# First layer of an expert tile with the tile's rows stationary: a copy on VectorE and four transposes in place of eight small products

## The chip, the cores and the metric

The kernel runs on one core of one Trainium2 chip. The metric is the time of one execution in microseconds, the median of several. The kernel before takes 1520.85 us (three runs, 1519.32 to 1523.46).

## The reference

One layer of a graph network over 6250 nodes of 256 features, everything in fp32: a sparse sum over 106250 edges, a linear attention over all nodes, and then the part that the change is in, a mixture of 16 experts of which each node takes two.

```python
xn = _layernorm(x, axis=-1)
x = x + _L0_gnn_ref(xn, src, dst, edge_weight, L0_gnn_weight) + _L0_mix_ref(xn[None], Wqkv, Wout, bout)[0]
...
gate_logits = x @ gate_w + gate_b
topk_vals, topk_idx = jax.lax.top_k(gate_logits, K)
topk_w = jax.nn.softmax(topk_vals, axis=-1)
h = jax.nn.relu(jnp.einsum('bsh,ehf->bsef', x, w1) + b1)
expert_out = jnp.einsum('bsef,efh->bseh', h, w2) + b2
sel = jnp.take_along_axis(expert_out, topk_idx[:, :, :, None], axis=2)
moe = jnp.sum(topk_w[..., None] * sel, axis=2)
y = x + moe
```

The experts' layers are 256 to 512 and 512 to 256. Their input is the layer-normed result of the first half.

## The kernel before

**The edges.** The 106250 edges lie in 70 batches of 12 tiles of 128. For each tile GpSimd issues one indirect DMA (L855) that gathers 128 rows of the normed table into `ring`, which holds two batches. TensorE sums a batch in `edges` (L1512) as soon as it has landed, ScalarE copies the sum (L992), TensorE puts it in place (L1521), VectorE adds it (L1116). GpSimd may gather batch b only when batch b-2 has been summed, so a late TensorE holds GpSimd up.

**The other work between batches.** `plan()` (L147) sets, once and by costs written in the code, what each engine does in the slot after each batch: attention (`kv`), the closing of node tiles (`mix`, `gate`), routing (`rank`, `slots`, `line`, `list`), the tiles of the experts (`moe`), and the final sum of node tiles (`fin1`, `fin2`). Each engine walks through the same slots in the same order. For an expert tile the plan counts 3.9 us of TensorE (L136).

**The expert tiles.** Routing gives each pair of a node and an expert a slot in a table in HBM; GpSimd scatters the rows there (L833), 128 slots of one expert make a tile. The tiles come in runs, one run after each routing: runs 0 to 4 (8, 16, 16, 16 and 12 tiles) and the first 13 tiles of run 5 lie between batches, the other 15 tiles of run 5 and the 25 of run 7 after the last batch; the short runs 6 and 8 are left out if they are empty. For tile g, in TensorE's order:

- `xg_turn(g + 1)`, L1636: two transposes of the next tile's rows; ScalarE copies them to SBUF (`xg_copy`, L946);
- `layer1(g)`, L1648: for each of the 4 blocks of 128 hidden features 2 products of 128 columns, the weights stationary and the transposed rows moving. So the result lies in PSUM already turned, features on the partitions, in one of two banks `hps`;
- `layer2(g - 1)`, L1661: 4 products of 256 columns with the turned hidden rows `hT` stationary.

ScalarE's `relu` (L967) adds the bias and makes `hT` (two buffers) from `hps`, in four instructions, as soon as layer 1 is done. VectorE adds the second bias (`moe_y`, L1445), and ScalarE issues the store of the result (`store_y`, L952). SyncE loads a tile's rows (L720) and, if the expert is another than three tiles before, both weights (L732 when `relu` three tiles before is done, L734 when `moe_y` is). Near the end of a part a tile can be empty (`where_taken`, L628): then its products and its `relu` are skipped.

**The end.** When the tiles of the first 42 node tiles are done, GpSimd picks their results out of HBM (`pick`, L846) and `fin1` (L1463 to L1475) and `fin2` (L1484 to L1493) close two node tiles at a time on VectorE. In `fin2` VectorE needs a square root that ScalarE makes (L986) and that stands in ScalarE's order behind the tile before it. The plan weaves 17 such pairs among the 25 tiles of run 7; 8 pairs follow after the last tile.

```python
            def moe(r, j):
                ...
                layer1(r, j)
                if j:
                    layer2(r, j - 1)
                if j + 1 == n:
                    layer2(r, j)
```

Of the kernel before, what the change touches and what calls it, by code (L numbers as in the profile page):

```python
# [9 lines left out]
ACT = mybir.ActivationFunctionType  # L10
AX = mybir.AxisListType

P = 128
N = 6250
D = 256
KD = D // P
# [25 lines left out]
E, F = 16, 512  # L42
FC = F // P
TS = 128
# [57 lines left out]
RUNS, VISITS = runs()  # L102
# [5 lines left out]
WB = 3  # L108
# [245 lines left out]
def gps_layer(nc, x, src, dst, first_dst, edge_w, gnn_w, wkv, wq, wout, bout, gate_w, gate_b,  # L354
# [5 lines left out]
    with ExitStack() as ctx:  # L360
# [3 lines left out]
        def sem(name):  # L364
            return ctx.enter_context(nc.semaphore(name))
# [30 lines left out]
        take = carve(room[:, :])  # L396
# [8 lines left out]
        take = carve(room[:, :])  # L405
        w1_sb = [take(W1ROW) for _ in range(WB)]
        w2_sb = [take(W2BROW) for _ in range(WB)]
        hT = [take(FC, TS) for _ in range(2)]
        xg = [take(D) for _ in range(XB)]
        xgT = [take(KD, TS) for _ in range(2)]  # L410

# [101 lines left out]
        gate_cols = [wide[1][:, 512 + D + i * E:512 + D + (i + 1) * E] for i in range(6)]  # L513
        mT, gnnT = [sq[:, i * 512:(i + 1) * 512].rearrange("p (j n) -> p j n", j=KD) for i in range(2)]
        boutT = ks[0][:, 0:D].rearrange("p (j n) -> p j n", j=KD)
        hps = [ps[:, 5, :], ps[:, 1, :]]
        xgps = ps[:, 6, 0:KD * TS]
        ops = ps[:, 7, 0:D]

# [73 lines left out]
        w1_in = sems("w1_in", WB)  # L593
        w2_in = sems("w2_in", WB)
        l1_done = sem("l1_done")
        relu_done = sem("relu_done")
        l2_done = sem("l2_done")
        y_done = sem("y_done")
# [12 lines left out]
        def after(eng, s, n):  # L611

            if n > 0:
                eng.wait_ge(s, n)
# [27 lines left out]
        def skip(eng, done, g0, n, each=1):  # L642

            if n:
                after(eng, done, each * g0)
                eng.sem_inc(done, each * n)
# [218 lines left out]
        def _(act):  # L865
# [88 lines left out]
            def moe(r, j):  # L954
                s, g0, n, _ = RUNS[r]
                g = g0 + j
                if j == 0:
                    act.wait_ge(listed, LISTS[s])
                    xg_copy(g)
                if j + 1 < n:  # L960
                    xg_copy(g + 1)

                def relu():
                    act.wait_ge(l1_done, g + 1)
                    after(act, l2_done, g - 1)
                    for f in range(FC):
                        last = act.activation(hT[g % 2][:, f, :], hps[g % 2][:, f * TS:(f + 1) * TS], ACT.Relu,  # L967
                                              bias=w1_sb[g % WB][:, KD * F + f:KD * F + f + 1])
                    last.then_inc(relu_done, 1)
                where_taken(act, r, j, relu, relu_done)  # L970
                if j:
                    store_y(r, j - 1)
                if j + 1 == n:
                    store_y(r, j)
# [22 lines left out]
        def _(dve):  # L997
# [443 lines left out]
            def moe_y(g):  # L1441
# [2 lines left out]
                after(dve, ys_out[g % 2], 16 * (g // 2))  # L1444
                dve.tensor_tensor(yo[g % 2], ops, w2_sb[g % WB][:, W2ROW:], ALU.add).then_inc(y_done, 1)  # L1445

            def moe(r, j):
                _, g0, n, _ = RUNS[r]
                if j:
                    moe_y(g0 + j - 1)  # L1450
                if j + 1 == n:
                    moe_y(g0 + j)

            def left_out(r):
                skip(dve, y_done, RUNS[r][1], RUNS[r][2])

            def fin1(f):
# [46 lines left out]
        def _(pe):  # L1504
# [134 lines left out]
            def layer1(r, j):  # L1639
                g = RUNS[r][1] + j  # L1640

                def products():
                    pe.wait_ge(xg_copied, g + 1)
                    after(pe, relu_done, g - 1)
                    pe.wait_ge(w1_in[g % WB], 16 * (g // WB + 1))
                    for f in range(FC):
                        for k in range(KD):
                            mm = pe.matmul(hps[g % 2][:, f * TS:(f + 1) * TS], w1_sb[g % WB][:, k * F + f * P:k * F + (f + 1) * P],  # L1648
                                           xgT[g % 2][:, k, :], start=(k == 0), stop=(k == KD - 1))
                    mm.then_inc(l1_done, 1)  # L1650
                where_taken(pe, r, j, products, l1_done)

            def layer2(r, j):
                g = RUNS[r][1] + j

                def products():
                    pe.wait_ge(relu_done, g + 1)
                    after(pe, y_done, g)
                    pe.wait_ge(w2_in[g % WB], 16 * (g // WB + 1))
                    for f in range(FC):  # L1660
                        mm = pe.matmul(ops, hT[g % 2][:, f, :], w2_sb[g % WB][:, f * D:(f + 1) * D], start=(f == 0), stop=(f == FC - 1))  # L1661
                    mm.then_inc(l2_done, 1)
                where_taken(pe, r, j, products, l2_done)

            def moe(r, j):
                s, g0, n, _ = RUNS[r]
                if j == 0:
                    pe.wait_ge(listed, LISTS[s])
                    xg_turn(g0)
                if j + 1 < n:  # L1670
                    xg_turn(g0 + j + 1)
                layer1(r, j)
                if j:
                    layer2(r, j - 1)
                if j + 1 == n:
                    layer2(r, j)

            def left_out(r):
                _, g0, n, _ = RUNS[r]
                skip(pe, xg_turned, g0, n)  # L1680
                skip(pe, l1_done, g0, n)
                skip(pe, l2_done, g0, n)

            pe.wait_ge(pool_consts, POOL_CONSTS)
# [78 lines left out]
```

## Time and profile before

| | us |
|---|---|
| median of 3 runs | 1520.85 |
| span of the profiled execution (its whole time is not given) | 2053.1 |
| of it PE busy / PE weight loads / DVE / ACT / POOL | 1168.8 / 848.9 / 651.8 / 406.3 / 1005.6 |
| last gather of an edge batch issued at | 1730.0 |
| layer 1 (L1648), 1904 passes, busy | 279.8 |
| layer 2 (L1661), 952 passes, busy | 270.5 |
| bytes moved by DMA | 323.09 MB |

PE is TensorE, PEld its weight loads, DVE VectorE, ACT ScalarE, POOL GpSimd, SP SyncE; a q behind a name is the engine's queue of DMA issues. An fp32 product shows as two passes: 119 tiles x 8 products are 1904 rows of L1648. A transpose shows as one. The profiled execution is 532 us longer than the runs without a profile.

### The profile page before, as it was taken

How to read it: one execution, taken by the hardware profiler on the slowest of the kernel's cores; microseconds unless marked ns; L12 is line 12 of the kernel's file. 1: busy time of each engine (PE TensorE's matmuls, PEld its weight loads, DVE VectorE, ACT ScalarE, POOL GpSimd, SP SyncE). 2: the span in 40 equal slices, each digit the busy share in tenths (PEclk: the TensorE clock that was granted, in tenths of full speed). 3: DMA queues.
4: the chain of work that ended last, by engine and by line, in shares of the span. 5: the costliest groups of instructions: out<-in, count | busy, mean ns of one | idle time of the engine just before them, and what ended most of it. 6: DMA issues, size and time to landing. Idle time of an engine off the chain costs nothing. (4 is left out here: it accounts for less than half of the span.)

```text
span 2053.1 us, 23292 instructions
## 1 busy us (share of the span) xinstructions
PE 1168.8 (57%) x6546; PEld 848.9 (41%) x6546; DVE 651.8 (32%) x2406; ACT 406.3 (20%) x1093; POOL 1005.6 (49%) x1094
## 2 busy tenths in 40 slices
PE   0278888976423767432576324773266367576681
PEld 0144444544313655221554213552154156465670
DVE  7144344333632212223112131122212222412568
ACT  4033232321101312000211001210021022222221
POOL 2746666664365244566254663446624643204634
PEclk9899999987755888655788666887577588887885
DMA  9345444432134656233574325653364274366784
GB/s 329 97 151 185 154 153 155 141 90 62 47 98 153 217 187 216 80 91 117 176 238 143 90 92 183 196 178 90 121 220 162 85 265 143 124 210 217 244 256 138
DMA packets 155049, 323.09 MB, mean 157 GB/s; under 512 B 24769, under 2 KB 97729, under 8 KB 154785
## 3 DMA queue, kind: packets, MB, share of 16 engines
q1 hardware_dynamic: 65760, 148.16, 21.9%
q0 software_dynamic: 49296, 134.68, 21.6%
q10 hardware_dynamic: 39856, 38.67, 5.6%
q8 instruction: 57, 0.93, 0.2%
q14 instruction: 80, 0.65, 0.1%
HBM read 257.06 MB, written 64.36 MB: 157 GB/s over the span
## 5 line engine op out<-in xcount | busy, mean ns | idle before, releaser
L855 POOL DMA_INDIRECT ring<-normed_rows,src_sb x831 | 797.9, 960 | 780.0 <-PE ps L1512 462.2
L1661 PE MATMUL ps<-room 128*128 128x256 f32 x952 | 270.5, 435 | 115.9 <-issue 79.9
L1648 PE MATMUL ps<-room 128*128 128x128 f32 x1904 | 279.8, 300 | 70.3 <-issue 58.6
L1648 PEld LDWEIGHTS ps<-room 128*128 128x128 f32 x1904 | 260.4, 214 | 80.0 <-issue 75.2
L1661 PEld LDWEIGHTS ps<-room 128*128 128x128 f32 x952 | 199.8, 221 | 155.4 <-issue 85.3
L1445 DVE TENSOR_TENSOR desk<-ps,room 128x256 f32<-128x256 f32 x121 | 51.3, 424 | 587.6 <-PE ps L1661 293.4
L1512 PE MATMUL ps<-ring,S 128*32 128x256 f32 x1680 | 145.6, 453 | 153.0 <-DVE aggT L1116 77.9
L1539 PE MATMUL ps<-room,tT 128*128 128x512 f32 x392 | 196.7, 644 | 11.4 <-issue 11.1
L967 ACT ACTIVATE room<-ps,room 128x128 f32<-128x128 f32 x476 | 136.1, 369 | 303.5 <-remote 201.2
L846 POOL DMA_INDIRECT ring<-results_by_slot,slot_i x98 | 96.5, 984 | 146.4 <-issue 80.9
L1512 PEld LDWEIGHTS ps<-ring,S 128*32 128x32 f32 x1680 | 60.8, 125 | 211.8 <-issue 188.4
L833 POOL DMA_INDIRECT rows_by_slot<-X,slot_i x98 | 96.1, 981 | 103.0 <-DVEq L1337 74.7
L1521 PE MATMUL ps<-Pm,accs 128*128 128x128 f32 x280 | 55.3, 329 | 138.1 <-ACT accs L992 106.2
L1529 PE MATMUL ps<-ident,X 128*128 128x128 f32 x196 | 48.7, 333 | 140.9 <-ACT tT L881 95.2
L992 ACT COPY accs<-ps 128x256 f32<-128x256 f32 x70 | 26.3, 376 | 495.4 <-remote 339.4
L1539 PEld LDWEIGHTS ps<-room,tT 128*128 128x128 f32 x392 | 77.5, 209 | 98.6 <-issue 98.5
L1133 DVE TENSOR_REDUCE kv_var<-room 128x16 f32<-128x1024 f32 x49 | 59.7, 1218 | 179.0 <-ACT room L901 130.3
L1636 PE MATMUL ps<-ident,room 128*128 128x128 f32 x242 | 53.6, 307 | 105.5 <-ACT room L946 69.3
L1521 PEld LDWEIGHTS ps<-Pm,accs 128*128 128x128 f32 x280 | 46.4, 227 | 156.5 <-ACT accs L992 120.3
L1529 PEld LDWEIGHTS ps<-ident,X 128*128 128x128 f32 x196 | 25.1, 161 | 166.2 <-ACT tT L881 103.6
L946 ACT COPY room<-ps 128x256 f32<-128x256 f32 x121 | 44.7, 370 | 235.2 <-remote 94.9
L1636 PEld LDWEIGHTS ps<-ident,room 128*128 128x128 f32 x242 | 33.5, 156 | 125.4 <-issue 115.8
(226 smaller groups left out, 1247.0 us busy)
## 6 DMA issues: line engine op xcount, KB each, us to landing
room<-in_w2b SPq DMA_DIRECT2D x92, 640.0 KB
room<-in_w1b SPq DMA_DIRECT2D x92, 514.0 KB
room<-rows_by_slot SPq DMA_DIRECT2D x121, 128.0 KB
results_by_slot<-desk ACTq DMA_DIRECT2D x121, 128.0 KB
rows_by_slot<-desk ACTq DMA_DIRECT2D x6, 2432.0 KB
ring<-normed_rows,src_sb POOLq DMA_INDIRECT x831
normed_rows<-X SPq DMA_DIRECT2D x7, 896.0 KB, 8.0
result<-ring SPq DMA_DIRECT2D x49, 128.0 KB
```

Source lines behind the costliest of these rows:

```text
L833: pool.indirect_dma_start(out=xs[p], out_offset=bass.IndirectOffsetOnAxis(ap=slot_i[:, k, q:q + 1], axis=0), in_=X2[:, q, :], in_offset=No ...
L846: pool.indirect_dma_start(out=pk[i][k][:, n, :], out_offset=None, in_=ys[p], in_offset=bass.IndirectOffsetOnAxis(ap=slot_i[:, k, q:q + 1], ...
L855: pool.indirect_dma_start(out=ring[:, b % 2 * BT + m, :], out_offset=None, in_=table, in_offset=bass.IndirectOffsetOnAxis(ap=src_sb[:, b * ...
L967: last = act.activation(hT[g % 2][:, f, :], hps[g % 2][:, f * TS:(f + 1) * TS], ACT.Relu, bias=w1_sb[g % WB][:, KD * F + f:KD * F + f + 1])
L1133: dve.tensor_reduce(kv_var[q % 2][:, :], sq.rearrange("p (h d) -> p h d", d=DH), AX.X, ALU.add).then_inc(kv_var_done, 1)
L1512: mm = pe.matmul(acc[w * W:(w + 1) * W, :], S[b % 2][:, m, :], ring[:, b % 2 * BT + m, :], start=(t == 0), stop=(t == GT - 1), skip_group_ ...
L1521: mm = pe.matmul(placed[:, k * P:(k + 1) * P], accs[:, k * P:(k + 1) * P], Pm[b % 2][:, :], start=True, stop=True, skip_group_check=True)
L1529: mm = pe.transpose(tps[:, k * P:(k + 1) * P], rows[:, k * P:(k + 1) * P], ident[:])
L1539: mm = pe.matmul(wide[q % 2][:, h * 512:(h + 1) * 512], tT[n % 2][:, k * P:(k + 1) * P], wkv_sb[:, k, h * 512:(h + 1) * 512], start=(k == ...
L1636: mm = pe.transpose(xgps[:, k * TS:(k + 1) * TS], xg[g % XB][:, k * P:(k + 1) * P], ident[:])
L1648: mm = pe.matmul(hps[g % 2][:, f * TS:(f + 1) * TS], w1_sb[g % WB][:, k * F + f * P:k * F + (f + 1) * P], xgT[g % 2][:, k, :], start=(k == ...
L1661: mm = pe.matmul(ops, hT[g % 2][:, f, :], w2_sb[g % WB][:, f * D:(f + 1) * D], start=(f == 0), stop=(f == FC - 1))
```

## The change

Layer 1 is turned round: the tile's transposed rows are stationary and the weight rows move, 512 columns at a time, so that 2 products take the place of 8. Their result has the tile's rows on the partitions. VectorE copies it from PSUM to SBUF (`h_copy`), TensorE turns it back with four transposes (`h_turn`), and `relu` works on what they leave. `hps`, `hT` and the new buffers are single. In the slot of a tile TensorE's order becomes `xg_turn(g + 1)`, `layer1(g)`, `layer2(g - 1)`, `h_turn(g)`; VectorE's `h_copy(g)` stands ahead of `moe_y(g - 1)`. The copy, the transposes and `relu` are done for an empty tile too.

```diff
+        hps = ps[:, 5, 0:F]
+        hTps = ps[:, 1, 0:FC * TS]
...
 # ScalarE, moe
-                def relu():
-                    act.wait_ge(l1_done, g + 1)
-                    after(act, l2_done, g - 1)
-                    for f in range(FC):
-                        last = act.activation(hT[g % 2][:, f, :], hps[g % 2][:, f * TS:(f + 1) * TS], ACT.Relu,
...
-                where_taken(act, r, j, relu, relu_done)
+                act.wait_ge(h_turned, g + 1)
+                after(act, l2_done, g)
+                for f in range(FC):
+                    last = act.activation(hT[:, f, :], hTps[:, f * TS:(f + 1) * TS], ACT.Relu,
+                                          bias=w1_sb[g % WB][:, KD * F + f:KD * F + f + 1])
+                last.then_inc(relu_done, 1)
...
 # VectorE
+            def h_copy(g):
+                dve.wait_ge(l1_done, g + 1)
+                after(dve, h_turned, g)
+                dve.tensor_copy(h_rows, hps).then_inc(h_copied, 1)
+
             def moe(r, j):
                 _, g0, n, _ = RUNS[r]
+                h_copy(g0 + j)
                 if j:
                     moe_y(g0 + j - 1)
...
 # TensorE, layer 1
-                    after(pe, relu_done, g - 1)
+                    after(pe, h_copied, g)
                     pe.wait_ge(w1_in[g % WB], 16 * (g // WB + 1))
-                    for f in range(FC):
-                        for k in range(KD):
-                            mm = pe.matmul(hps[g % 2][:, f * TS:(f + 1) * TS], w1_sb[g % WB][:, k * F + f * P:k * F + (f + 1) * P],
-                                           xgT[g % 2][:, k, :], start=(k == 0), stop=(k == KD - 1))
+                    for k in range(KD):
+                        mm = pe.matmul(hps, xgT[g % 2][:, k, :], w1_sb[g % WB][:, k * F:(k + 1) * F],
+                                       start=(k == 0), stop=(k == KD - 1))
...
+            def h_turn(g):
+                pe.wait_ge(h_copied, g + 1)
+                after(pe, relu_done, g)
+                for f in range(FC):
+                    mm = pe.transpose(hTps[:, f * TS:(f + 1) * TS], h_rows[:, f * P:(f + 1) * P], ident[:])
+                mm.then_inc(h_turned, 1)
...
                 if j:
                     layer2(r, j - 1)
+                h_turn(g0 + j)
                 if j + 1 == n:
                     layer2(r, j)
```

TensorE's order at the first tile after the last routing's list, in run 5, before (L1636 turns the next tile's rows, L1648 is layer 1, L1661 layer 2 of the tile before):

```order
L1636 MATMUL ps<-ident,room 128x128 [waits xg_copied,xg_in2]
L1636 MATMUL ps<-ident,room 128x128
L1648 MATMUL ps<-room 128x128 [waits w1_in1,relu_done,xg_copied]
L1648 MATMUL ps<-room 128x128 x7
L1661 MATMUL ps<-room 128x256 [waits w2_in0,y_done,relu_done]
L1661 MATMUL ps<-room 128x256 x3
```

and with the change (L1645 turns the rows, L1656 is layer 1, L1676 layer 2, L1665 the new transposes):

```order
L1645 MATMUL ps<-ident,room 128x128 [waits xg_copied,xg_in2]
L1645 MATMUL ps<-ident,room 128x128
L1656 MATMUL ps<-room 128x512 [waits w1_in1,h_copied,xg_copied]
L1656 MATMUL ps<-room 128x512
L1676 MATMUL ps<-room 128x256 [waits w2_in0,y_done,relu_done]
L1676 MATMUL ps<-room 128x256 x3
L1665 MATMUL ps<-ident,room 128x128 [waits relu_done,h_copied]
L1665 MATMUL ps<-ident,room 128x128 x3
```

Between layer 2 and the next tile's transposes TensorE now waits for VectorE's copy. VectorE's order among the last tiles with `fin2` and `fin1` between two results, before (L1445 is `moe_y`):

```order
L1445 TENSOR_TENSOR desk<-ps,room 128x256 [waits ys_out1,w2_in0,l2_done]
L1484 SCALAR_TENSOR_TENSOR ring<-ring,f_mv,gamma_b 128x256 [waits f_stats]
L1484 SCALAR_TENSOR_TENSOR ring<-ring,f_mv,gamma_b 128x256
L1487 RECIPROCAL f_r<-f_r 128x2 [waits f_std]
L1493 SCALAR_TENSOR_TENSOR ring<-ring,f_r,aggT 128x256 [waits f_scaled,f_recip]
L1493 SCALAR_TENSOR_TENSOR ring<-ring,f_r,aggT 128x256 [waits f_scaled]
L1445 TENSOR_TENSOR desk<-ps,room 128x256 [waits ys_out0,w2_in1,l2_done]
```

and with the change (L1452 is the copy, L1447 `moe_y`):

```order
L1452 COPY room<-ps 128x512 [waits h_turned,l1_done]
L1447 TENSOR_TENSOR desk<-ps,room 128x256 [waits ys_out1,w2_in2,l2_done]
L1493 SCALAR_TENSOR_TENSOR ring<-ring,f_mv,gamma_b 128x256 [waits f_stats]
L1493 SCALAR_TENSOR_TENSOR ring<-ring,f_mv,gamma_b 128x256
L1496 RECIPROCAL f_r<-f_r 128x2 [waits f_std]
L1502 SCALAR_TENSOR_TENSOR ring<-ring,f_r,aggT 128x256 [waits f_scaled,f_recip]
L1502 SCALAR_TENSOR_TENSOR ring<-ring,f_r,aggT 128x256 [waits f_scaled]
```

The copy stands behind all closing work of the slot before. ScalarE's order at the same place, before (L967 is `relu`, L986 the root for `fin2`):

```order
L946 COPY room<-ps 128x256 [waits l1_done,xg_turned]
L967 ACTIVATE room<-ps,room 128x128 [waits l2_done,l1_done]
L967 ACTIVATE room<-ps,room 128x128 x3
L950 TENSOR_LOAD ttab
L950 ISA x2
L952 ISA [waits y_done]
L952 DMA results_by_slot<-desk 128x256
L986 ACTIVATE f_r<-f_mv,eps_t 128x2 [waits f_stats]
```

and with the change:

```order
L950 COPY room<-ps 128x256 [waits l1_done,xg_turned]
L970 ACTIVATE room<-ps,room 128x128 [waits l2_done,h_turned]
L970 ACTIVATE room<-ps,room 128x128 x3
L954 TENSOR_LOAD ttab
L954 ISA x2
L956 ISA [waits y_done]
L956 DMA results_by_slot<-desk 128x256
L988 ACTIVATE f_r<-f_mv,eps_t 128x2 [waits f_stats]
```

The order is the same, but the root stands behind a `relu` that now waits for the transposes, and so for layer 2 of the tile before.

## Rows read from the trace of the kernel before

**Rows 1.** The page's first line.

```profile
span 2053.1 us, 23292 instructions
```

**Rows 2.** One line: the gathers; ns min/median/max, first and last start.

```profile
L855 POOL DMA_INDIRECT ring<-normed_rows,src_sb x831: 940/947/2857, 53.5 to 1730.0; - x167
```

**Rows 3.** The page's groups: the scatters; busy us, mean ns, idle before.

```profile
L833 POOL DMA_INDIRECT rows_by_slot<-X,slot_i x98 | 96.1, 981 | 103.0 <-DVEq L1337 74.7
```

**Rows 4.** Who waited for whom, whole span: us, times, longest.

```profile
POOL ring L855 <- PE ps L1512: 462.2, 40, 32.4
```

**Rows 5.** Timeline, PE and POOL: start, us, engine, [idle before].

```profile
1031.02 0.27 PE L1648 MATMUL ps<-room 128*128 128x128 f32 x1 [1.04 <-issue]
...
1033.90 0.37 PE L1648 MATMUL ps<-room 128*128 128x128 f32 x1 [1.05 <-issue]
...
1045.82 0.94 POOL L855 DMA_INDIRECT ring<-normed_rows,src_sb  x1 [0.30 <-issue]
```

**Rows 6.** Timeline, one undisturbed tile of run 5 after the last batch.

```profile
1803.73 0.38 PE L1636 MATMUL ps<-ident,room 128*128 128x128 f32 x2
...
1803.95 1.95 PE L1648 MATMUL ps<-room 128*128 128x128 f32 x16
...
1805.73 1.89 PE L1661 MATMUL ps<-room 128*128 128x256 f32 x8
...
1805.93 1.14 ACT L967 ACTIVATE room<-ps,room 128x128 f32<-128x128 f32 x4 [0.57 <-PE ps L1648]
...
1807.46 0.38 PE L1636 MATMUL ps<-ident,room 128*128 128x128 f32 x2
```

**Rows 7.** Timeline, attention: eight passes of 512 columns and what follows.

```profile
274.56 3.60 PE L1539 MATMUL ps<-room,tT 128*128 128x512 f32 x8
...
278.00 1.05 PE L1547 MATMUL ps<-room 128*128 128x128 f32 x8
```

**Rows 8.** One line: VectorE on 512 columns of PSUM.

```profile
L1125 DVE TENSOR_TENSOR room<-ps,kv_s x49: 690/691/692, 109.1 to 447.8; 128x512 f32<-128x512 f32 x49
```

**Rows 9.** Timeline, PE at a batch of edges among tiles.

```profile
1019.19 1.50 PE L1512 MATMUL ps<-ring,S 128*32 128x256 f32 x24
1020.62 0.44 PE L1636 MATMUL ps<-ident,room 128*128 128x128 f32 x2
...
1024.41 0.61 PE L1521 MATMUL ps<-Pm,accs 128*128 128x128 f32 x4
1024.86 0.38 PE L1636 MATMUL ps<-ident,room 128*128 128x128 f32 x2
```

**Rows 10.** Stretches: busy us, clock, DMA share, GB/s.

```profile
710.00:720.00 10.00, 9.91 (x74) 9.43 (x75) 0.64 (x2) 4.43 (x15) 0.00 (x0) 1.00 0.94 328
...
1843.00:2004.00 161.00, 110.25 (x635) 96.67 (x635) 76.33 (x227) 40.39 (x137) 74.37 (x76) 0.83 0.75 240
```

**Rows 11.** Timeline, from the end of run 5 to run 7.

```profile
1836.10 1.97 PE L1661 MATMUL ps<-room 128*128 128x256 f32 x8 [0.34 <-DVE desk L1445]
...
1842.96 0.34 SPq L732 DMA_DIRECT2D room<-in_w1b  x1
...
1849.86 0.45 PE L1636 MATMUL ps<-ident,room 128*128 128x128 f32 x1 [11.80 <-DMA room<-rows_by_slot]
```

**Rows 12.** Timeline, a tile of run 7 with `fin2` and `fin1`.

```profile
1957.12 0.42 DVE L1445 TENSOR_TENSOR desk<-ps,room 128x256 f32<-128x256 f32 x1 [1.26 <-PE ps L1661]
...
1957.47 0.87 DVE L1484 SCALAR_TENSOR_TENSOR ring<-ring,f_mv,gamma_b 128x256 f32<-128x256 f32 x2
...
1958.14 0.29 ACT L986 ACTIVATE f_r<-f_mv,eps_t 128x2 f32<-128x2 f32 x1 [1.60 <-DVE desk L1445]
...
1958.47 0.17 DVE L1487 RECIPROCAL f_r<-f_r 128x2 f32<-128x2 f32 x1
```

**Rows 13.** The chain that ended last: two starts of `fin2`, one pair apart.

```profile
2016.56 0.55 DVE ring L1484 x2
...
2020.93 0.55 DVE ring L1484 x2
```

More of the change, by code:

```diff
@@ L407, in gps_layer @@
         w2_sb = [take(W2BROW) for _ in range(WB)]
-        hT = [take(FC, TS) for _ in range(2)]
+        hT = take(FC, TS)
+        h_rows = take(F)
         xg = [take(D) for _ in range(XB)]
@@ L515, in gps_layer @@
         boutT = ks[0][:, 0:D].rearrange("p (j n) -> p j n", j=KD)
-        hps = [ps[:, 5, :], ps[:, 1, :]]
+        hps = ps[:, 5, 0:F]
+        hTps = ps[:, 1, 0:FC * TS]
         xgps = ps[:, 6, 0:KD * TS]
@@ L595, in gps_layer @@
         l1_done = sem("l1_done")
+        h_copied = sem("h_copied")
+        h_turned = sem("h_turned")
         relu_done = sem("relu_done")
@@ L961, in moe @@
                     xg_copy(g + 1)
-                def relu():
-                    act.wait_ge(l1_done, g + 1)
-                    after(act, l2_done, g - 1)
-                    for f in range(FC):
-                        last = act.activation(hT[g % 2][:, f, :], hps[g % 2][:, f * TS:(f + 1) * TS], ACT.Relu,
-                                              bias=w1_sb[g % WB][:, KD * F + f:KD * F + f + 1])
-                    last.then_inc(relu_done, 1)
-                where_taken(act, r, j, relu, relu_done)
+                act.wait_ge(h_turned, g + 1)
[4 more added lines that the diff above has]
+                last.then_inc(relu_done, 1)
                 if j:
@@ L1454, in left_out @@
             def left_out(r):
+                skip(dve, h_copied, RUNS[r][1], RUNS[r][2])
                 skip(dve, y_done, RUNS[r][1], RUNS[r][2])
@@ L1660, in products @@
                     for f in range(FC):
-                        mm = pe.matmul(ops, hT[g % 2][:, f, :], w2_sb[g % WB][:, f * D:(f + 1) * D], start=(f == 0), stop=(f == FC - 1))
+                        mm = pe.matmul(ops, hT[:, f, :], w2_sb[g % WB][:, f * D:(f + 1) * D], start=(f == 0), stop=(f == FC - 1))
                     mm.then_inc(l2_done, 1)
@@ L1681, in left_out @@
                 skip(pe, l1_done, g0, n)
+                skip(pe, h_turned, g0, n)
                 skip(pe, l2_done, g0, n)
```

## The prediction

> **What bounds the kernel now.** I read the page, then the waits, then the timeline of single tiles, then stretches with the DMA share, and last the chain that ended last.
>
> The span is 2053.1 us [rows 1], 532 us more than the median of 1520.85. The timeline shows why the two differ: again and again TensorE starts one small pass and then sits for about a microsecond with no releaser [rows 5], though all operands are there. In undisturbed stretches nothing of this kind occurs. So I take every price from undisturbed stretches, keep the profile's stalls out of the sum, and add the sum to the median.
>
> Up to the last gather GpSimd sets the floor. A gather takes 0.95 us and follows the one before by 0.30 us [rows 2, 5], so 1.25 us each. From 53.5 us on come 831 gathers and 84 of the 98 scatters [rows 2, 3]: 53.5 + 915 x 1.25 = 1197 us, while the profile has its last gather at 1730.0 [rows 2]. The 462.2 us for which GpSimd waited for TensorE [rows 4] are mostly the stalls, passed on. What is left of the median is 324 us; the profile has 323 us behind the last gather, with stalls in it. So perhaps 50 to 75 us of real waits lie before the last gather, the rest is the end phase: 15 tiles of run 5, 25 of run 7 with the closing pairs, then pure closing on VectorE, 4.37 us a pair [rows 13].
>
> An undisturbed tile takes 1807.46 - 1803.73 = 3.73 us of TensorE: 0.22 for two transposes, 1.78 for layer 1 (16 passes of 0.111), 1.73 for layer 2 [rows 6]. A batch of edges takes 1.43 and 0.45 us [rows 9]. Three tiles and a batch are 13.1 us against 12 x 1.25 = 15.0 on GpSimd: TensorE has 1.9 us spare. The DMA engines have none: with tiles back to back they are 94% busy at 328 GB/s without any gather beside [rows 10].
>
> **Layer 1 and the transposes on TensorE.** Eight passes of 512 columns take 278.00 - 274.56 = 3.44 us, 0.43 each [rows 7]. The new layer 1 has 4: 1.72 us in place of 1.78. As many columns stream as before (4 x 512, 16 x 128), and the weight loads were hidden already. The four transposes take 4 x 0.11 = 0.44 us at the pitch of L1636 [rows 6]. Net +0.37 us a tile, 4.10 in place of 3.73.
>
> The trace's 0.43 us for a 512-column pass is 4 times its 0.11 for 128. The Trainium skill (TensorE: Matmul & The Clock Gate, Back-to-back issue gap) gives, for a stream of load and product, about 81 ns at 128 columns and 131 ns at 512; by that layer 1 would fall from 1.30 to 0.52 us and the change would win 0.45 us a tile even with its transposes at 81 ns. The rows contradict it for fp32, so the sum goes by the rows.
>
> **The copy on VectorE.** The trace has no plain copy of 512 columns from PSUM; VectorE's work of that size takes 0.69 us [rows 8], and 256 columns take 0.42 [rows 12]. I take 0.69, between 0.42 and 0.69. With VectorE idle it hides under layer 2 of the tile before (1.73 us). The same holds for `relu`: it now starts after the transposes, 1.14 us [rows 6], and has 0.22 + 1.72 us until the next layer 2. So among tiles without closing work only the 0.37 us shows.
>
> **SyncE.** The w1 load three tiles on waits for `relu`, which is now about 1.2 us later than the `moe_y` for which the w2 load ahead of it in the queue waits. The lead of this load falls from about 7.2 to 7.0 us of a period that has grown to 12.3. I count nothing; its cover is the two tiles' weights already queued. ScalarE's store of the result stands behind `relu` too, about 1.1 us later, covered by the second `yo`.
>
> **Sum by stretch.**
> - Before the last gather, 81 tiles. 13.1 + 3 x 0.37 = 14.2 us is still under 15.0, and the weights queue at the DMA engines. Cost only where TensorE is late already: the five to seven tiles at the head of each of 5 bursts, and waits for the copy behind `gate`. Bounds 0 and 81 x 0.37 + 5 x 3 = 45; I take 5, near the covered end, because both covers show in rows.
> - Run 5 after the last gather: 13 tiles x 0.37 = 5.
> - End of run 5: two empty tiles, for which nothing was done after the last layer 2 [rows 11]. Now two rounds of transposes (0.44) with a `relu` (1.14 and handover) between them stand ahead of SyncE's loads for run 7, for which TensorE waits 11.8 us [rows 11]: +3. The first tile of run 7 has no layer 2 to hide the copy: +1.
> - Run 7 with closing work. Now VectorE needs 4.37 + 0.42 = 4.8 us for a tile with a full pair [rows 12, 13], about 4.3 on the mean over the pattern (two full pairs, a `fin2`, a `fin1` in four tiles). But 161 us x 240 GB/s = 38.6 MB move there [rows 10], at 328 GB/s 118 us, 4.9 us a tile: the DMA engines bound it. With the change three engines stand in a ring. The copy comes after all closing work of the slot before; then transposes 0.45, `relu` 1.19, the store's issue 0.6, the root 0.33 until VectorE can go on with the reciprocal: 2.6 us, where now it is 1.35 from `moe_y`'s start and 0.8 of it worked [rows 12]. A full pair then takes 0.7 + 2.6 + 3.57 (a pair without its first 0.8) = 6.9 us. Stepping through four tiles gives 22.5 us, 5.6 a tile, 24 tiles 134 us. Against 118: +16; against 24 x 4.3: +31; if the DMA engines still hide it, 0. I take 15, since the DMA bound is the one that rows show.
> - Last tile: its `relu` and transposes are bare, 0.44 + 1.3: +2. The 8 closing pairs after it stay.
>
> Sum 5 + 5 + 3 + 1 + 15 + 2 = +31 us: **1552 us**.
>
> **Rivals.**
> 1. *Covered, not slower.* The DMA engines hold run 7 and the bursts at more than 4.9 us a tile, and each copy falls into a wait. It decides this way if the ring (5.6 by my stepping) in truth takes 4.9 or less, as it would if the closing pairs catch up in the slots without one. Then only end effects of a few us stay, partly made up: 1521 to 1525. For it: 94% DMA share at full pitch [rows 10]. Against: over run 7 the share is 0.75, stalls included. Chance 0.13.
> 2. *The gathers are held too.* The 50 to 75 us of waits before the last gather are TensorE's lateness, not DMA. Then 81 x 0.37 and the waits behind `gate` and at heads of runs come in full: +45 in place of 5, and run 7 at +16: 1592; half-way 1572. For it: GpSimd waits for TensorE alone [rows 4]. Against: 14.2 us fits into 15.0. Chance 0.20.
> 3. *Faster.* The transposes run while TensorE waits for weights, so that only layer 1's 0.06 us counts: 119 x 0.06 = 7 us, 1514. It needs TensorE idle just where the copy is ready, in all stretches, and no ring at the closing pairs. Chance 0.05. The rule of the Trainium skill on the issue gap would carry it further; the trace speaks against it.
>
> **How the numbers follow.** The forecast (1530 to 1572) has 0.62, the rivals 0.13, 0.20 and 0.05. A measurement of this kernel tells about 0.3%, 4.6 us, from no change. Faster 0.05, same 0.13, slower 0.82. The range goes from 1522, which leaves out the third and part of the first rival, to 1588, which leaves out the far end of the second.
>
> **What would show it.** Right: L1648's 1904 rows become 476 of about 0.43 us pitch; four new transposes of 0.11; a copy of about 0.69 us, 121 times; an undisturbed tile at 4.1 us; in run 7 VectorE waits about 1 us for the root between the two parts of `fin2`, and TensorE waits for the copy ahead of its transposes. The profile's span may fall though the time grows, since its stalls go with TensorE's rows and a tile has fewer. Wrong: a tile still at 3.7 us; no wait for the copy in run 7; a time under 1525 would say that the DMA engines or GpSimd cover all, one over 1575 that the gathers are held.

## The result and the profile after

The changed kernel takes 1568.77 us (median of 4 runs, 1568.12 to 1571.03), the kernel before beside it on the same chip 1522.15 us (4 runs, 1519.32 to 1525.73). The ratio is 1.0294, with a 95% interval of 1.0263 to 1.0325: 45 us slower, where 31 were forecast. The direction was right, the time lies inside the range, and the forecast is 17 us too low. One run of all those told of here was slow (1596.09 us, in experiment 12), and no ratio counts it, though the median there does.

The profiled execution of the changed kernel has no stalls: its span is 1566.8 us, 2 us below the median. So its stretches can be read as they are. For those of the kernel before, a second profiled execution without stalls was taken in the first experiment (span 1524.4). From here on "before" means that one.

The page's groups, first of the changed kernel (line engine op, shapes | busy us, mean ns | idle before it, releaser):

```profile
L1656 PE MATMUL ps<-room 128*128 128x512 f32 x476 | 250.9, 654 | 6.9 <-DMA room<-in_w1b 4.3
L1452 DVE COPY room<-ps 128x512 f32<-128x512 f32 x121 | 83.2, 688 | 249.5 <-PE ps L1656 248.9
```

then of before:

```profile
L1648 PE MATMUL ps<-room 128*128 128x128 f32 x1904 | 257.8, 294 | 26.7 <-DMA room<-in_w1b 26.1
```

The 1904 passes are 476, and they save 6.9 us of busy time. The copy takes 688 ns. The last number of each row of layer 1 tells how close the DMA engines were: before, TensorE waited 26.1 us for w1 weights at this line, now 4.3. The four transposes a tile, as one answer on their line shows them (min/median/max ns, who it waited for, us and times):

```profile
L1665 PE MATMUL ps<-ident,room x484: 272/273/477, 499.9 to 1522.1; 128*128 128x128 f32 x162
...
  DVE room L1452: 70.1, 40
```

The gathers, which answer to [rows 2], end later, and GpSimd waits more for TensorE ([rows 4] show the stalled profile). Of the changed kernel, the line of the gathers, then who waited for whom over the whole span:

```profile
L859 POOL DMA_INDIRECT ring<-normed_rows,src_sb x831: 940/946/2865, 53.7 to 1268.3; - x167
...
POOL ring L859 <- PE ps L1521: 62.6, 15, 15.7
```

and of before:

```profile
L855 POOL DMA_INDIRECT ring<-normed_rows,src_sb x831: 941/946/2858, 53.4 to 1254.1; - x167
...
POOL ring L855 <- PE ps L1512: 44.6, 10, 16.3
```

From the starts of such instructions each profile can be cut in stretches: to the last gather, to the last `moe_y` of run 5 (the 96th), to the first turned rows of run 7, to the last `moe_y`, to the end.

| us | last gather at | rest of run 5 | to run 7 | run 7 | closing | span |
|---|---|---|---|---|---|---|
| before | 1254.1 | 97.8 | 9.6 | 121.8 | 41.1 | 1524.4 |
| changed | 1268.3 | 107.0 | 10.4 | 139.9 | 41.2 | 1566.8 |
| difference | +14.2 | +9.2 | +0.8 | +18.1 | +0.1 | +42.4 |
| forecast | +5 | +5 | +4 | +17 | 0 | +31 |

Each row is one profiled execution. Profiles of the experiments below that have the same form in a stretch tell how far it scatters: the last gather lies at 1250.2 to 1255.7 in the old form (experiments 1, 4 and 10) and at 1268.3 to 1273.3 in the new one (the changed kernel, 2, 6 and 9), run 7 takes 121.2 to 123.7 us in the old form and 139.9 to 142.2 in the new one. So the first difference is 13 to 23 us, and nothing under about 2.5 us in run 7 can be told from scatter.

Run 7 of the changed kernel, as [rows 10] show it of before: stretch, us, busy of each engine, granted clock, DMA share, GB/s. The second stretch holds two tiles with a pair.

```profile
1385.00:1525.00 140.00, 116.72 (x449) 75.60 (x450) 93.51 (x257) 41.36 (x142) 73.86 (x77) 0.91 0.86 274
...
1452.00:1465.00 13.00, 9.06 (x40) 5.95 (x39) 10.73 (x31) 3.27 (x12) 9.96 (x11) 1.00 0.68 201
```

The same stretch of before:

```profile
1361.00:1483.00 122.00, 102.48 (x650) 91.72 (x650) 78.58 (x232) 41.76 (x142) 72.89 (x76) 0.95 0.92 313
```

Without stalls the kernel before has its DMA engines 92% busy at 313 GB/s through all of run 7; TensorE has time over there. Changed, TensorE's granted clock over run 7 is 0.91 in place of 0.95 (the last section comes back to it), and the DMA share falls to 0.86 and in the tiles with pairs to 0.68: something else has become the bound. The timeline of one such tile, which answers to [rows 12], shows what: VectorE (DVE), ScalarE (ACT) and TensorE (PE) follow each other in a ring.

```profile
1452.33 0.60 PE L1665 MATMUL ps<-ident,room 128*128 128x128 f32 x4
...
1452.97 0.88 ACT L970 ACTIVATE room<-ps,room 128x128 f32<-128x128 f32 x3 [2.60 <-PE ps L1665]
...
1453.65 0.34 ACTq L956 DMA_DIRECT2D results_by_slot<-desk  x1
...
1454.05 0.30 ACT L988 ACTIVATE f_r<-f_mv,eps_t 128x2 f32<-128x2 f32 x1
...
1454.37 0.17 DVE L1496 RECIPROCAL f_r<-f_r 128x2 f32<-128x2 f32 x1 [0.63 <-ACT f_r L988]
...
1457.83 0.67 DVE L1452 COPY room<-ps 128x512 f32<-128x512 f32 x1
...
1458.56 0.66 PE L1665 MATMUL ps<-ident,room 128*128 128x128 f32 x4 [1.97 <-DVE room L1452]
...
1460.66 0.17 DVE L1496 RECIPROCAL f_r<-f_r 128x2 f32<-128x2 f32 x1 [1.04 <-ACT f_r L988]
...
1464.85 0.66 PE L1665 MATMUL ps<-ident,room 128*128 128x128 f32 x4 [1.97 <-DVE room L1452]
```

The transposes start `relu`, the root stands behind `relu` and the store, VectorE waits for the root, works off the pair, and only then makes the next copy, for which TensorE sits 1.97 us. One round is 1464.85 - 1458.56 = 6.29 us. Over run 7, from the first tile's turned rows to the last's in the same list of starts, a tile takes 5.3 us (before: 4.6).

### The profile page after: what moved, and what is told of

It reads as the page before. It is cut to its first block and busy times, and to the rows that moved or that the text cites. A ratio compares the mean times of both kernels' runs of the same rounds, so it can differ in the third digit from the quotient of the medians.

```text
span 1566.8 us, 21700 instructions
## 1 busy us (share of the span) xinstructions
PE 1093.6 (70%) x5602; PEld 699.5 (45%) x5602; DVE 732.6 (47%) x2527; ACT 411.3 (26%) x1101; POOL 1003.7 (64%) x1094
## 3 DMA queue, kind: packets, MB, share of 16 engines
q0 software_dynamic: 49296, 134.68, 27.5%
## 5 line engine op out<-in xcount | busy, mean ns | idle before, releaser
L1521 PE MATMUL ps<-ring,S 128*32 128x256 f32 x1680 | 132.0, 457 | 178.8 <-DMA ring<-normed_rows,src_sb 121.6
L1656 PE MATMUL ps<-room 128*128 128x512 f32 x476 | 250.9, 654 | 6.9 <-DMA room<-in_w1b 4.3
L1676 PE MATMUL ps<-room 128*128 128x256 f32 x952 | 229.9, 385 | 8.5 <-ACT room L970 8.4
L1676 PEld LDWEIGHTS ps<-room 128*128 128x128 f32 x952 | 184.7, 195 | 87.9 <-issue 42.7
L1452 DVE COPY room<-ps 128x512 f32<-128x512 f32 x121 | 83.2, 688 | 249.5 <-PE ps L1656 248.9
L1548 PE MATMUL ps<-room,tT 128*128 128x512 f32 x392 | 182.3, 609 | 0.0
L1656 PEld LDWEIGHTS ps<-room 128*128 128x128 f32 x476 | 89.7, 210 | 75.2 <-issue 71.9
L1645 PE MATMUL ps<-ident,room 128*128 128x128 f32 x242 | 53.4, 306 | 80.7 <-issue 45.2
L1447 DVE TENSOR_TENSOR desk<-ps,room 128x256 f32<-128x256 f32 x121 | 51.3, 424 | 120.1 <-PE ps L1676 118.6
L1548 PEld LDWEIGHTS ps<-room,tT 128*128 128x128 f32 x392 | 73.6, 198 | 73.8 <-issue 73.8
L1665 PE MATMUL ps<-ident,room 128*128 128x128 f32 x484 | 76.6, 283 | 28.5 <-DVE room L1452 27.1
L1665 PEld LDWEIGHTS ps<-ident,room 128*128 128x128 f32 x484 | 60.5, 144 | 52.9 <-DVE room L1452 43.0
L905 ACT ACTIVATE room<-ps 128x1024 f32<-128x1024 f32 x49 | 50.2, 1024 | 124.4 <-PE ps L1548 124.4
L1645 PEld LDWEIGHTS ps<-ident,room 128*128 128x128 f32 x242 | 31.0, 153 | 92.6 <-issue 71.9
```

The costliest lines, as they stand in the source:

```text
L1452: dve.tensor_copy(h_rows, hps).then_inc(h_copied, 1)
L1521: mm = pe.matmul(acc[w * W:(w + 1) * W, :], S[b % 2][:, m, :], ring[:, b % 2 * BT + m, :], start=(t == 0), stop=(t == GT - 1), skip_group_ ...
L1548: mm = pe.matmul(wide[q % 2][:, h * 512:(h + 1) * 512], tT[n % 2][:, k * P:(k + 1) * P], wkv_sb[:, k, h * 512:(h + 1) * 512], start=(k == ...
L1645: mm = pe.transpose(xgps[:, k * TS:(k + 1) * TS], xg[g % XB][:, k * P:(k + 1) * P], ident[:])
L1656: mm = pe.matmul(hps, xgT[g % 2][:, k, :], w1_sb[g % WB][:, k * F:(k + 1) * F], start=(k == 0), stop=(k == KD - 1))
L1665: mm = pe.transpose(hTps[:, f * TS:(f + 1) * TS], h_rows[:, f * P:(f + 1) * P], ident[:])
```

## The experiments

Each is compared with runs of the kernel before on the same chip; differences in us are its ratio less 1, times the median of before there. The plain differences of the two medians lie up to 2.4 us off these.

**1. The kernel before again, for a profile without stalls.** No edit.

> The kernel before, unchanged, profiled again, to have a profile without the stalls of TensorE that lengthened the first one by 532 us. Expected by every theory: 1520 to 1526 us, and in the profile a span near it. The theory that DMA bounds run 7 expects its 25 tiles to take about 118 to 125 us with waits for loads in them; the theory that VectorE and TensorE bound it expects about 24 x 4.3 = 103 us plus few waits. The theory that the gathers are already held by TensorE expects GpSimd's waits for L1512 to sum to 50 us or more.

Measured: ratio 0.9989 (0.9966 to 1.0012), span 1524.4 at a median of 1526.05. The stalls were a property of the first profiled execution. The last gather is at 1254.1, against the floor of 1197 in the prediction. Run 7 takes 121.8 us at a DMA share of 0.92, as the theory that DMA bounds it expects. GpSimd waits 44.6 us for the sums of edges, just under the 50 that the theory of held gathers asked for: it was held for most of the 57 us above the floor, and the run decides for neither side alone.

**2 to 4. The new form in some runs only.** Three kernels with both forms, chosen by run: the head has the new form in runs 0 to 4, the middle in 5 and 6, the last in 7 and 8.

```diff
+TURNED_RUNS = (0, 1, 2, 3, 4)
...
+                if r in TURNED_RUNS:
+                    h_copy(g0 + j)
```

and the same choice at `relu`, `layer1`, `h_turn` and `layer2`.

> Only the tiles of runs 0 to 4 (68 tiles, all before the last gather) take the new form; later tiles have the old one. Ring theory (the loss is in run 7, where the copy, relu and the root for the closing pairs stand in a ring): +5 to +13 us. Rival (TensorE already holds the gathers, and 0.37 us a tile comes in full there): +25 us or more. Everything covered before the last gather: 0.

> Only the tiles of run 5 (13 before the last gather, 15 after it, two of them empty) and of the left-out run 6 take the new form. Both theories: 13 x 0.37 = 5 us after the last gather, 3 for the two empty tiles, 1 to 3 before it: +8 to +11 us.

> Only the 25 tiles of run 7 (and the left-out run 8) take the new form. Ring theory: +18 to +33 us, the largest of the three parts, with full closing pairs at 6.2 us a tile where the kernel before has 4.8. Rival: 25 x 0.37 + 3 = +12 us. If the sum of the three parts is the whole +46, the parts are independent.

Measured: head 1.0086 (1.0061 to 1.0112), +13 us; middle 1.0049 (1.0031 to 1.0067), +7.5; last 1.0102 (1.0073 to 1.0130), +15.6. Together 36 us of the 45 (by plain medians 42 of 47); each part is known to 3 to 4 us, so whether the parts add up to the whole is known to several us only. The last is below its expectation of 18 to 33, and its interval of 11 to 20 us holds the rival's 12 too; it is the profile that tells them apart, and that is of the slowest of its six runs. The profiles put the time where the new form is: the head has its last gather at 1268.5 and all else within 1.5 us of before, the last has run 7 at 142.2 us (+20.4) and all else within 1.6. So the loss before the last gather is not a consequence of anything later. The middle's profile shows the rest of run 5 at 111.8 us, 4.8 more than the changed kernel has there, with a span of 1540.5 against a median of 1536.03; how exactly its term is to be split stays open by a few us.

**5. The transposes alone.** The kernel before, with four more transposes a tile after layer 2, into the free bank; their result is not used. No copy, no new wait.

```diff
                 if j:
                     layer2(r, j - 1)
+                after(pe, relu_done, g0 + j)
+                for f in range(FC):
+                    pe.transpose(hps[(g0 + j + 1) % 2][:, f * TS:(f + 1) * TS], upper[:], ident[:])
```

> The kernel before, with four more transposes (of a constant, into the bank that is free until the next tile) at the end of each tile's slot on TensorE: 0.44 us of TensorE a tile and no new wait for another engine. What it adds to the computation is not used. If TensorE's time as such is small (GpSimd covers it before the last gather, the DMA engines cover it in run 7), then 13 to 15 x 0.44 = 6 us in run 5, 0 to 4 elsewhere: +6 to +10 us. If TensorE's time per tile is what the change costs, 119 x 0.44 = +52 us, or at least +20.

Measured: 1539.82 us, ratio 1.0086 (1.0056 to 1.0115), +13 us, more than the theory gave. By stretch: last gather at 1266.8 (+12.7), rest of run 5 101.6 (+3.8), run 7 120.9 (-0.9), closing the same. This is the most telling run. Before the last gather bare TensorE time brings nearly all of the changed kernel's +14.2. In run 7 the same transposes, 25 x 0.44 = 11 us of TensorE, cost nothing that can be told from scatter: the waits for the DMA engines give way. A part is given back by the clock, 0.98 there against 0.95 before; TensorE is busy 110.32 us over the 121, 7.8 more than before. What run 7 loses with the change, +18.1, is therefore the copy, its waits, and the clock that TensorE loses in them.

**6. The root ahead of `relu`.** The changed kernel, with ScalarE's root for `fin2` ahead of the tile in the last slot.

```diff
+            roots_first = list(SLOTS[NB])
+            for i in range(1, len(roots_first)):
+                if roots_first[i][0] == "fin2" and roots_first[i - 1][0] == "moe":
+                    roots_first[i - 1:i + 1] = [roots_first[i], roots_first[i - 1]]
```

> The changed kernel, but after the last gather ScalarE makes the root for fin2 ahead of the tile (its copy and relu) that stands before it in the plan. Ring theory: VectorE's 16 waits for the root in run 7 (15.6 us in the changed kernel's trace) go, and most of it comes back: 1557 to 1562 us. Rival, that the copy's place behind the closing work alone decides: the wait moves to the next copy, under 3 us come back.

Measured: 1557.66 us, ratio 1.0199 (1.0168 to 1.0230), 11 us less than the change by the medians and 14 by the ratios, within what the theory of the ring expected. Run 7 takes 128.3 us, +6.5 instead of +18.1; the stretches ahead of it are not faster (last gather 1270.7). Cutting one link of the ring gives back 12 us of the 18.

**7. The copy on ScalarE.** The changed kernel, with `h_copy` ahead of `relu` on ScalarE instead of on VectorE.

```diff
+                act.wait_ge(l1_done, g + 1)
+                after(act, h_turned, g)
+                act.copy(h_rows, hps).then_inc(h_copied, 1)
...
-                h_copy(g0 + j)
```

> The changed kernel, with the copy of 512 columns on ScalarE (0.59 us) in place of VectorE, ahead of relu in its order. Theory that TensorE's loss is the wait for a copy queued behind gate and behind the closing pairs on VectorE: TensorE's 70 us of weight-load waits for the copy go; 8 to 10 us come back before the last gather and 6 to 10 in run 7: 1548 to 1556 us. Rival (TensorE's own 0.37 us a tile): nothing comes back, 1567 or more.

Measured: 1546.19 us, ratio 1.0149 (1.0121 to 1.0176), 22 us less than the change. More came back than the 14 to 20 us expected, and elsewhere: 16 us in run 7, which takes 123.9 (+2.1), and only 3 before the last gather, which is at 1265.4 (+11.3); the rest of run 5 takes 103.7 (+5.9). TensorE had waited 23.5 us for the copy before the last gather, and these waits cost little there. The copy takes less on ScalarE too, and TensorE's wait for it goes. The groups of this kernel, as above:

```profile
L969 ACT COPY room<-ps 128x512 f32<-128x512 f32 x121 | 70.9, 586 | 112.5 <-PE ps L1658 111.9
...
L1667 PE MATMUL ps<-ident,room 128*128 128x128 f32 x484 | 73.2, 274 | 8.0 <-ACT room L969 7.9
```

In run 7 it is mainly what the copy is queued behind that costs: ScalarE has nothing long ahead of it. This run also takes 0.69 us a tile of work off VectorE and does not part the two. Experiment 6 bounds that: the copy is still VectorE's there, and run 7 is 4.4 us longer than here. The new buffers and `hps` and `hT` are single in this run as well, so whatever that costs in run 7 lies within its +2.1.

**8. Both.** The copy on ScalarE and the root ahead of `relu`.

> The changed kernel with both: the copy on ScalarE and the root ahead. If both waits are parts of one ring in run 7, the two together bring back less than their sum: 1543 to 1550 us; what is left over the kernel before is TensorE's 0.37 us a tile in run 5, the empty tiles and the bare ends of runs, 15 to 20 us. If they are independent: 1538 or less.

Measured: 1550.27 us, ratio 1.0163 (1.0138 to 1.0189): no better than experiment 7, and not the 1538 of independent waits. The times of 7 and 8 differ by less than their intervals, but in the profiles run 7 takes 131.0 us here, 7 more. With the root first, ScalarE waits for VectorE's variance before it may copy. Who waited for whom in run 7 (us, times, longest), of experiment 8:

```profile
ACT f_r L992 <- DVE f_mv L1490: 29.8, 14, 3.1
...
PEld ps L1671 <- ACT room L969: 17.5, 16, 2.2
```

and of experiment 7:

```profile
DVE f_r L1498 <- ACT f_r L992: 6.2, 8, 2.0
PEld ps L1667 <- ACT room L969: 1.8, 2, 1.5
```

The wait for the copy is 17.5 us in one and 1.8 in the other, though the copy is on the same engine: the root that was moved ahead holds it.

**9. Empty tiles skipped.** The changed kernel, with the transposes and `relu` of an empty tile under `where_taken`, as before the change.

```diff
+                def relu():
...
+                where_taken(act, r, j, relu, relu_done)
...
+                where_taken(pe, r, j, turns, h_turned)
```

> The changed kernel, with the transposes and relu of an empty tile skipped as the products are (the copy stays). Expected by every theory: the two empty tiles at the end of run 5 cost 3 us there, so 1564 to 1567 us, and the stretch from the last result of run 5's full tiles to run 7's first rows as in the kernel before. If it is still 1569, the end of run 5 was not on the path.

Measured: 1571.11 us, ratio 1.0293 (1.0264 to 1.0321): no gain, against 2 to 5 us expected. The stretch between run 5 and run 7 is 9.3 us instead of 10.4, so the term is worth about 1 us in this stretch, too little for the time to show.

**10. The root ahead in the kernel before.**

> The kernel before with the same move of ScalarE's root as in the changed kernel: its VectorE waits for the root only once, 1.4 us, so nothing to win: 1519 to 1526 us. A gain of over 5 us would say that the place of the root costs by itself, whatever the form of layer 1.

Measured: 1524.51 us, ratio 0.9993 (0.9973 to 1.0014), run 7 at 121.2 us. Before the change there is no ring to cut: VectorE waits 1.4 us for the root in all of run 7, the changed kernel 15.6.

**11 and 12. Where before the last gather do the transposes cost?** Experiment 5 with its transposes in some tiles only.

```diff
+                if 1 <= r <= 4 and j < 9:
```

in 11, and in 12

```diff
+                if r == 0 or (1 <= r <= 4 and j >= 9):
```

> The kernel before with the four extra transposes in only the first nine tiles of runs 1 to 4 (36 tiles, 15.8 us of TensorE). Theory: the transposes of the earlier run cost time before the last gather only where TensorE is already behind GpSimd, at the heads of the runs, where the mixing products (5.1 us) stand among the tiles. Then these 36 tiles bring most of the 12.7 us that all tiles brought before the last gather: last gather 1259 to 1265, time +7 to +11 us. Rival: each tile costs alike wherever it stands, 12.7 x 36 / 81 = +5.6 us, last gather 1258 or less. Second rival: the cost lies in the last tiles of the runs, then +0 to +3.

> The kernel before with the four extra transposes in all tiles of run 0 and the tiles from the tenth on in runs 1 to 4 (32 tiles, 14.1 us of TensorE), and in no others. By the theory of the heads these are nearly hidden by GpSimd's gathers: last gather 1252 to 1258, time +0 to +4 us, of which up to 3 in run 0. Rival that each tile costs alike: 12.7 x 32 / 81 = +5.0 us. Rival that the ends of the runs cost: +7 to +10.

Measured: heads 1532.73 us, 1.0041 (1.0011 to 1.0070), +6.2 us, last gather in the profile 1254.2; the others 1534.49 us, 1.0046 (1.0015 to 1.0077), +7.0 us, last gather 1262.6. The theory of the heads is not borne out: both last gathers lie outside what it expected, on the side against it. By the ratios each tile costs about alike, 0.2 us of its 0.44, as the first rival expected, and the two sum to the 13 of experiment 5; but the intervals (+2 to +11 and +2 to +12 us) are wide enough for the other theories, so that alike is the likeliest and not shown. The profile of the heads does not show its +6; it is of the fastest of its ten runs, and the last gather scatters by some 5 us from profile to profile.

Where the gathers are held shows batch by batch, in the time from a batch's first gather to the next one's (us; numbers are the batches'):

| batch | before | changed | transposes alone | 11, heads | 12, others |
|---|---|---|---|---|---|
| 28 | 20.6 | 27.5 | 24.9 | 21.6 | 26.7 |
| 31 | 15.0 | 18.7 | 18.3 | 16.4 | 16.4 |
| 44 | 15.1 | 17.9 | 15.9 | 15.1 | 17.0 |
| 55 | 15.0 | 16.7 | 17.0 | 15.1 | 15.2 |

Of the 69 spacings 57 differ by less than 0.5 us between before and the change. So most slots are covered, as the prediction had it; the loss is in a few. The four rows shown make 15.1 us; the others beyond 0.5 us go both ways (the largest, batch 66 with +2.9, spreads from 17.4 to 20.9 us among kernels without the new form). Batch 28 waits for a sum of edges that stands in TensorE's order behind run 0 and the first tiles of run 1; run 0 is in experiment 12, and so is most of this loss (its 26.7; without the new form there it spreads from 20.3 to 23.6, in experiments 10 and 4). Batch 31 falls in a slot with mixing products. TensorE there, before:

```profile
592.66 1.08 PE L1612 MATMUL ps<-gnn_sb,aggT 128*128 128x272 f32 x4
593.57 0.61 PE L1521 MATMUL ps<-Pm,accs 128*128 128x128 f32 x4
594.02 0.38 PE L1636 MATMUL ps<-ident,room 128*128 128x128 f32 x2
...
605.31 1.50 PE L1512 MATMUL ps<-ring,S 128*32 128x256 f32 x24
```

and changed, from one batch of edges to the next:

```profile
593.76 1.50 PE L1521 MATMUL ps<-ring,S 128*32 128x256 f32 x24
595.19 0.44 PE L1538 MATMUL ps<-ident,X 128*128 128x128 f32 x2
...
596.37 1.15 PE L1618 MATMUL ps<-M,tT 128*128 128x288 f32 x4
597.35 1.08 PE L1621 MATMUL ps<-gnn_sb,aggT 128*128 128x272 f32 x4
...
600.15 0.61 PE L1530 MATMUL ps<-Pm,accs 128*128 128x128 f32 x4
...
613.23 0.66 PE L1665 MATMUL ps<-ident,room 128*128 128x128 f32 x4 [0.61 <-DVE room L1452]
613.82 1.50 PE L1521 MATMUL ps<-ring,S 128*32 128x256 f32 x24
```

This slot holds 600.15 - 595.19 = 4.96 us of mixing products beside the three tiles. It takes 20.06 us of TensorE, against 15.0 for GpSimd's twelve gathers. With the two slots before it (14.33 each, from the same lines' starts) TensorE needs 48.7 us for three batches where GpSimd needs 45: the 3.7 us by which batch 31 is longer. Before, the same three slots take TensorE 13.69, 13.23 and 18.14, which is 45.05 us: there was no slack to hide anything in.

## Why the prediction was right in sign and short in size

**Prices.** Right. Layer 1 is four passes with a pitch of 0.43 us: in the timeline it starts at 1452.98 and layer 2 follows at 1454.70, 1.72 us. The transposes take 0.44, the copy 0.688 (0.69 forecast), and an undisturbed tile 4.10 us, between 1448.23 and 1452.33 on line L1665. The rule of the Trainium skill (TensorE: Matmul & The Clock Gate, Back-to-back issue gap), by which 512 columns go at about 131 ns, does not hold for these fp32 passes: with 512 columns streaming, layer 1 still takes 0.43 us a pass.

**Before the last gather: 5 taken, 14.2 measured.** This is the step that failed. The prediction compared "13.1 + 3 x 0.37 = 14.2 us" of TensorE with 15.0 of GpSimd and found it covered. That batch of 13.1 us has no other work in it; slots with mixing products take 5 us more, and from run 0 on sums of edges are late already (GpSimd idles 5.9 us ahead of batch 29 before the change, 12.8 after it). What stands in its place is measured: the transposes alone bring +12.7 here, and the head runs of the new form +14.4. The other part of the term, waits for the copy behind `gate`, is there with 23.5 us, but moving the copy to ScalarE gives only 3 us back. "Near the covered end" was the wrong place in the bounds of 0 and 45; the second rival had the mechanism, with 45 far too much and its half-way point of 1572 close to the result.

**Run 5 behind the last gather: 5 and 3 taken, 9.2 measured.** 3.8 of it is transposes (experiment 5), near the 5. Between 1311 and 1315 there is a wait that the prediction did not have in this stretch: the copy stands on VectorE behind the routing chain. The chain's last step ahead of the copy, the copy and the transposes of the changed kernel:

```profile
1314.06 0.17 DVE L1342 TENSOR_TENSOR prob<-prob 128x7 f32<-128x7 f32 x1
1314.16 0.69 DVE L1452 COPY room<-ps 128x512 f32<-128x512 f32 x1
...
1314.91 1.11 PE L1665 MATMUL ps<-ident,room 128*128 128x128 f32 x4 [3.74 <-DVE room L1452]
```

From the rows turned at 1304.74 to those at 1322.11 two tiles take 17.37 us; the same two take 12.23 with transposes alone (1303.60 to 1315.83). The 5.1 us between them, the wait of 3.74 and the slower passes behind it, are nearly all that the changed kernel has above experiment 5 in this stretch (5.4). The order shown ahead of the prediction had this place; its wait was not priced. With the copy on ScalarE the two tiles take 12.2 again (1302.33 to 1314.57), but the stretch keeps +5.9; what it loses there instead is not settled.

**To run 7: 3 and 1 taken, 0.8 measured.** The empty tiles' rounds cost TensorE time that lies inside the wait for the rows of run 7: TensorE still waits 11.02 us for them after its last transposes, before 12.05 after its last product. From the end of the last product to these rows it is 13.41 us against 12.05, so the rounds cost 1.4 us in all, part of it in the stretch before. The term was mis-sized by half or more, and experiment 9 gives back no time that can be told.

**Run 7: 15 and 2 taken, 18.1 measured.** Right in mechanism; the size is in part luck. A tile with a full pair takes 6.29 us (6.9 forecast), 5.3 on the mean (5.6), against 4.6 before (4.9 as the DMA bound): 24 x 0.66 = 15.9 us. The other 2.2 us lie behind the last tile's turned rows, as forecast. But the two sides of the difference were both 7 us too long and cancel: 24 tiles take 127.0 us, not 134, and before 111.1, not 118. And the sum had no term for the clock: TensorE is busy 14.2 us more than before over run 7, while the new form adds 25 x 0.37 = 9; its granted clock is lower there, 0.91 against 0.95. Both rows named as signs are there: VectorE waits for the root (15.6 us in 16 times) and TensorE for the copy. Cutting the ring at either of two places gives most of the time back, 11.6 us and 16.0, together more than the 18.1 that there are to win (experiments 6 and 7); and where both are changed the copy waits for the root again (8).

**The stalls.** Reading them as a property of that one profiled execution, and adding the sum to the median, was right: two later profiles of these kernels have none and their spans lie within 2 us of the medians. Had the sum gone by shares of the 2053 us, every term would have been off.

**The rivals.** "Covered" is refuted except for the transposes in run 7 (experiment 5). "The gathers are held too" holds for a third of its price. "Faster" needs TensorE idle in all stretches; the waits for w1 weights at layer 1, 26.1 us before and 4.3 now, show that such idle time was there, and that it did not suffice.

## What to carry to other kernels

Before moving work onto an engine's queue, read what stands ahead of it there at each place, not what the engine's busy share is: the same copy costs 22 us more on VectorE, which is 47% busy, than on ScalarE, for the most part because it waits behind closing and routing work. Compare an engine's added time with its slack slot by slot: a batch with room to spare says nothing of the slot that holds other work besides. And where several engines hand on to each other in a ring, test it by cutting two different links: if what the cuts give back one at a time sums to more than the whole, the two waits are parts of one chain and not two costs.

## What the hardware showed that was not expected

The wait for the copy in run 5 costs more than its own length, by TensorE's clock. Four stretches of the changed kernel, columns as above, the granted clock third from the end: layer 2 ahead of the wait, the wait, layer 1 behind it, and what follows.

```profile
1308.60:1311.20 2.60, 2.57 (x9) 1.82 (x7) 2.07 (x13) 0.00 (x0) 0.00 (x0) 0.73 0.00 0
...
1311.20:1314.90 3.70, 0.00 (x0) 0.00 (x0) 3.06 (x17) 0.00 (x0) 0.92 (x1) 0.80 0.00 0
1316.20:1319.60 3.40, 3.40 (x6) 1.40 (x5) 0.00 (x0) 1.35 (x5) 2.49 (x4) 0.50 0.66 170
...
1320.50:1322.00 1.50, 1.50 (x11) 1.30 (x9) 0.22 (x2) 0.00 (x0) 1.20 (x2) 1.00 0.56 216
```

TensorE had sat 7.95 us for the routing before and had run layer 1 at 0.50, its lower level of 1.2 GHz; in layer 2 it comes back (0.73). Then it idles 3.7 us and is at 0.50 again: the next layer 1 takes 1319.66 - 1316.24 = 3.42 us instead of 1.72. With transposes alone there is no wait at this place, and the next layer 1 runs at 1.00. The waits in run 7 go either way. Those of 1.97 us shown above have no such fall beside them: the clock is 1.00 over 1452 to 1465. This one has, though TensorE had been busy for all of the 11 us from 1399 to 1410 at 1.00:

```profile
1410.77 1.89 PE L1676 MATMUL ps<-room 128*128 128x256 f32 x8
1416.00 1.12 PE L1665 MATMUL ps<-ident,room 128*128 128x128 f32 x4 [3.34 <-DVE room L1452]
1416.90 0.64 PE L1645 MATMUL ps<-ident,room 128*128 128x128 f32 x2
1417.33 2.82 PE L1656 MATMUL ps<-room 128*128 128x512 f32 x4
1419.99 1.89 PE L1676 MATMUL ps<-room 128*128 128x256 f32 x8
```

Layer 1 takes 1419.99 - 1417.33 = 2.66 us in place of 1.72, at 0.60 over 1416 to 1420. A low clock shortly before is thus not needed. And behind a wait of 1.93 us, at 1496.09, the clock is 0.72 over 1496 to 1500. So the runs do not give the length of wait that brings a fall; they show that such a wait can cost 1 to 2 us beyond itself.

The other surprise is that 11 us of transposes in run 7 cost nothing that shows on an engine that is 84% busy there (102.48 of 122 us before): the share does not tell that its remaining waits, most of them for DMA, move aside, nor that the clock rises as they shrink (0.95 to 0.98).
